# Attribute groups loaded further ahead, and edge rows added by VectorE: a graph pipeline on one core

## The reference

```
edge_in = concat(h[row], h[col], edge_attr)            # 256 + 256 + 64
msg     = relu(edge_in @ W1.T + b1) @ W2.T + b2
agg     = segment_sum(msg, row)
h'      = GRU(agg, h)                                  # W_ih, W_hh, b_ih, b_hh
x       = x + h'
```

## Time and profile before

| | us |
|---|---|
| median of 3 runs | 9225.33 (9208.56 to 9230.66) |
| the profiled execution, its own time | 9230.41 |
| its span in the trace | 9228.7 |
| TensorE busy | 5520.2 (60% of the span) |
| VectorE busy | 4108.1 (45%) |
| GpSimd busy | 4089.5 (44%) |
| ScalarE busy | 1858.0 (20%) |
| mean granted TensorE clock | 0.774 of full |

### The profile page before, as it was taken

How to read it: one execution, slowest core, us unless ns; L and a number is a source line. 1 busy time by engine, 2 the same in 40 slices (tenths; PEclk the granted TensorE clock), 3 DMA queues, 4 the chain that set the end, 5 groups by cost and what they waited for, 6 DMA issues and landing times. The chain is left out here.

```text
span 9228.7 us, 92213 instructions
## 1 busy us (share of the span) xinstructions
PE 5520.2 (60%) x22602; PEld 3755.3 (41%) x22603; DVE 4108.1 (45%) x11767; ACT 1858.0 (20%) x3938; POOL 4089.5 (44%) x3696
## 2 busy tenths in 40 slices
PE   2666477666557656658894665429964554553562
PEld 1344355455434434445552444325642232232551
DVE  9000577655631244444455777871133343343003
ACT  1222000011111122222112444312321221120120
POOL 5763466577646648870002444200016636642331
PEclk9999788777668877779796777658986676675785
DMA  2443111233325467760001222100013323320552
GB/s 52 86 87 87 37 22 20 48 97 98 79 86 153 132 102 138 138 126 1 8 10 49 62 60 62 31 1 14 14 35 89 90 51 92 89 62 15 169 170 91
DMA packets 495939, 657.70 MB, mean 71 GB/s; under 512 B 177294, under 2 KB 378098, under 8 KB 495669
## 3 DMA queue, kind: packets, MB, share of 16 engines
q0 software_dynamic: 229440, 352.40, 18.0%
q1 hardware_dynamic: 266228, 302.44, 11.0%
HBM read 512.00 MB, written 141.59 MB: 71 GB/s over the span
## 5 line engine op out<-in xcount | busy, mean ns | idle before, releaser
L739 POOL DMA_INDIRECT conv_rows<-rows_b,end_dst x832 | 837.2, 1006 | 1517.4 <-SPq L2406 1147.3
L771 DVE TENSOR_TENSOR acc<-acc,ps 125x256 f32 (+2 forms) x2080 | 881.3, 424 | 1199.7 <-issue 370.6
L739 POOL DMA_INDIRECT gat_rows<-rows,end_dst x832 | 869.1, 1045 | 627.3 <-issue 233.0
L2452 PE MATMUL ps<-conv_rows,conv_weight_of 128*125 128x256 f32 x1664 | 629.6, 512 | 674.9 <-issue 310.0
L739 POOL DMA_INDIRECT hyp_rows<-rows,end_dst x416 | 415.1, 998 | 993.7 <-SPq L1967 492.5
L1581 POOL DMA_INDIRECT mpnn_rows<-rows_b,end_src x416 | 657.4, 1580 | 261.7 <-DMA mpnn_rows<-records_src 139.5
L2452 PEld LDWEIGHTS ps<-conv_rows,conv_weight_of 128*125 128x125 f32 x1664 | 346.1, 239 | 958.4 <-issue 519.8
L1298 PE MATMUL ps<-xT,experts_w 128*128 128x500 f32 (+1 forms) x1344 | 560.7, 555 | 186.2 <-DMA experts_w<-in_L_ffn_w 162.2
L309 POOL DMA_INDIRECT records_src<-by_src_edge_stage,by_src_edge_slot x400 | 521.3, 1303 | 336.6 <-DMA by_src_edge_stage<-edge_rows 224.1
L474 POOL DMA_INDIRECT records_dst<-front_back,front_dst_addr x400 | 494.9, 1237 | 269.4 <-issue 269.4
L878 DVE TENSOR_REDUCE gat_red<-ps 125x8 f32<-125x1024 f32 x416 | 503.9, 1217 | 197.0 <-remote 127.8
(11 more groups left out here) (559 smaller groups left out, 9886.9 us busy)
## 6 DMA issues: line engine op xcount, KB each, us to landing
mlp_w<-in_L_ffn_w SPq DMA_DIRECT2D x136, 512.0 KB
mpnn_rows<-records_src SPq DMA_DIRECT2D x52, 1024.0 KB
edge_rows<-front_edge_ring SPq DMA_DIRECT2D x100, 503.9 KB
by_src_edge_stage<-edge_rows SPq DMA_DIRECT2D x100, 503.9 KB
gat_rows<-rows,end_dst POOLq DMA_INDIRECT x832
conv_rows<-rows_b,end_dst POOLq DMA_INDIRECT x832
front_attr<-in_edge_attr SPq DMA_DIRECT2D x100, 125.0 KB
rows_b<-acc SPq DMA_DIRECT2D x3, 3125.0 KB
```

Of the source, the lines that this page charges most:

```text
L739: pool.indirect_dma_start(out=rows[:, n % U, t, :], out_offset=None, in_=table, in_offset=bass.IndirectOffsetOnAxis(ap=ends[:, n * G + t:n ...
L771: dve.tensor_tensor(here, here, S.ps[0:P, t % banks, 0:width], ALU.add).then_inc(added, 1)
L2452: pe.matmul(S.ps[0:P, t, 0:D], weight_of[:, q.slot, t, :], rows[:, q.slot, t, :], start=True, stop=True).then_inc(summed, 1)
```

## The change

In the front part the attribute buffers go from 3 to AR = 6 and the ring from 2 to ER = 3. SyncE loads group g + 6 ahead of the store of group g, not group g + 3 behind it.

In the message loop the edge rows have a buffer of their own, `mpnn_edge`, of two halves of four tiles (512 KB each in a transfer); there are two loads a group, each waiting for `joined` of the same half of the group before. GpSimd uses `gather_groups` and adds nothing; it no longer waits for edge rows. VectorE's message t adds the product to the edge buffer. Behind each four messages a new stage, `join`, adds the edge half to the gathered rows (128 x 4 x 256), and ScalarE's relu waits for the join. SyncE no longer waits for the memsets (`ready`) before its first load.

```diff
--- before.py
+++ after.py
@@ -153,6 +153,8 @@
 SC = EC + PADC
 SG = 4
 AG = 4
+AR = 6
+ER = 3
 
 
 def turning(nc, S, A, sb, names):
@@ -378,10 +380,10 @@
             sem(x) for x in ("keys_ready", "staged", "scattered", "back_in", "taken"))
 
 
-        attr, attr_t = sb("attr", [P, 3, AG, ED]), sb("attr_t", [ED, 2, AG, P])
-        ring = sb("edge_ring", [P, 2, AG, EW])
-        attr_in = [sem(f"attr_in{r}") for r in range(3)]
-        rows_stored = [sem(f"edge_rows_stored{r}") for r in range(2)]
+        attr, attr_t = sb("attr", [P, AR, AG, ED]), sb("attr_t", [ED, 2, AG, P])
+        ring = sb("edge_ring", [P, ER, AG, EW])
+        attr_in = [sem(f"attr_in{r}") for r in range(AR)]
+        rows_stored = [sem(f"edge_rows_stored{r}") for r in range(ER)]
         attr_turned, attr_out, edge_product, edge_out = (
             sem(x) for x in ("attr_turned", "attr_out", "edge_product", "edge_out"))
         w1c = turned["L1_gnn_W1"][0:ED, 4, :]
@@ -406,7 +408,7 @@
                 for dst_, src_ in loads[:len(TURNED)]:
                     sp.dma_start(dst_, src_).then_inc(loaded, 16)
                 attributes = A["edge_attr_64"].rearrange("(p t) c -> p t c", p=P)
-                for g in range(3):
+                for g in range(AR):
                     sp.dma_start(attr[:, g], attributes[:, g * AG:(g + 1) * AG, :]).then_inc(attr_in[g], 16)
                 sp.dma_start(S.x[:, :, :], A["x"].rearrange("(t p) d -> p t d", p=P)).then_inc(x_in, 16)
                 sp.dma_start(w[:], A["L0_gnn_W"].rearrange("(k p) f -> p k f", p=128)).then_inc(gat_in, 16)
@@ -420,12 +422,12 @@
 
                 out = S.edge_rows.rearrange("(p t) w -> p t w", p=P)
                 for g in range(AGROUPS):
+                    if g + AR < AGROUPS:
+                        sp.wait_ge(attr_turned, g + 1)
+                        sp.dma_start(attr[:, g % AR], attributes[:, (g + AR) * AG:(g + AR + 1) * AG, :])\
+                            .then_inc(attr_in[g % AR], 16)
                     sp.wait_ge(edge_out, 3 * (g + 1))
-                    sp.dma_start(out[:, g * AG:(g + 1) * AG, :], ring[:, g % 2]).then_inc(rows_stored[g % 2], 16)
-                    if g + 3 < AGROUPS:
-                        sp.wait_ge(attr_turned, g + 1)
-                        sp.dma_start(attr[:, g % 3], attributes[:, (g + 3) * AG:(g + 4) * AG, :])\
-                            .then_inc(attr_in[g % 3], 16)
+                    sp.dma_start(out[:, g * AG:(g + 1) * AG, :], ring[:, g % ER]).then_inc(rows_stored[g % ER], 16)
                 sp.wait_ge(blocks_copied, len(jobs))
                 for to, from_ in stores:
                     sp.dma_start(to, from_).then_inc(stored, 16)
@@ -438,8 +440,8 @@
                 sp.wait_ge(back_in, 16)
                 sp.wait_ge(nodes_stored, 32)
                 sp.wait_ge(stored, 16 * len(stores))
-                for r in range(2):
-                    sp.wait_ge(rows_stored[r], 16 * AGROUPS // 2)
+                for r in range(ER):
+                    sp.wait_ge(rows_stored[r], 16 * len(range(r, AGROUPS, ER)))
 
             @block.gpsimd
             def _(pool):
@@ -491,11 +493,11 @@
 
                 for g in range(AGROUPS + 1):
                     if g < AGROUPS:
-                        pe.wait_ge(attr_in[g % 3], 16 * (g // 3 + 1))
+                        pe.wait_ge(attr_in[g % AR], 16 * (g // AR + 1))
                         if g >= 2:
                             pe.wait_ge(attr_out, g - 1)
                         for t in range(AG):
-                            ins = pe.transpose(S.ps[0:ED, g % 2, t * P:(t + 1) * P], attr[:, g % 3, t, :],
+                            ins = pe.transpose(S.ps[0:ED, g % 2, t * P:(t + 1) * P], attr[:, g % AR, t, :],
                                                S.ident[0:P, 0:P])
                         ins.then_inc(attr_turned, 1)
                     if g >= 1:
@@ -549,13 +551,13 @@
                            .then_inc(attr_out, 1)
                     if g >= 1:
                         h = g - 1
-                        if h >= 2:
-                            act.wait_ge(rows_stored[h % 2], 16 * (h // 2))
+                        if h >= ER:
+                            act.wait_ge(rows_stored[h % ER], 16 * (h // ER))
                         at = slice(h * AG, (h + 1) * AG)
-                        act.copy(ring[:, h % 2, :, 0:2], stage[:, at, 0:2]).then_inc(edge_out, 1)
+                        act.copy(ring[:, h % ER, :, 0:2], stage[:, at, 0:2]).then_inc(edge_out, 1)
                         for t in range(0, AG, 2):
                             act.wait_ge(edge_product, 2 * h + t // 2 + 1)
-                            act.copy(ring[:, h % 2, t:t + 2, 2:EW],
+                            act.copy(ring[:, h % ER, t:t + 2, 2:EW],
                                      S.ps[0:P, 2 + 2 * (h % 2) + t // 2, :].rearrange("p (t d) -> p t d", d=D))\
                                .then_inc(edge_out, 1)
 
@@ -1547,10 +1549,10 @@
                 dve.wait_ge(taken, 2)
 
         gathered = [sem(f"gathered{u}") for u in range(U)]
-        edges_in = [sem(f"edges_in{u}") for u in range(U)]
-        (go, selected, turned, turned_out, widened, products, messages, rectified, summed, added, ready) = (
-            sem(x) for x in ("go", "selected", "turned", "turned_out", "widened", "products", "messages", "rectified",
-                             "summed", "added", "ready"))
+        edges_in = [sem(f"edges_in{u}") for u in range(2)]
+        (go, selected, turned, turned_out, widened, products, messages, joined, rectified, summed, added, ready) = (
+            sem(x) for x in ("go", "selected", "turned", "turned_out", "widened", "products", "messages", "joined",
+                             "rectified", "summed", "added", "ready"))
         with nc.Block() as block, ExitStack() as ctx:
             def mb(what, shape, dt=F32):
                 return ctx.enter_context(nc.sbuf_tensor(f"mpnn_{what}", shape, dt))
@@ -1558,30 +1560,24 @@
             rows = mb("rows", [128, U, G, D + 1])
             onehot_b, onehot = mb("onehot_b", [128, 2, G, P], BF16), mb("onehot", [128, 2, G, P])
             onehot_t = mb("onehot_t", [P, 2, G, 128], BF16)
+            edge = mb("edge", [128, 2, G // 2, D])
             view = S.records["src"].rearrange("(p t) w -> p t w", p=128)
 
             PB = 4
 
             @block.sync
             def _(sp):
-                sp.wait_ge(ready, 2)
-
                 def load(q):
-                    if q.since(U):
-                        sp.wait_ge(summed, (q.n - U + 1) * G)
-                    sp.dma_start(rows[:, q.slot, :, 0:D], view[:, q.tiles(), 2:EW]).then_inc(edges_in[q.slot], 16)
+                    for half in range(2):
+                        if q.since(1):
+                            sp.wait_ge(joined, 2 * q.n - 1 + half)
+                        tiles = bass.ds(q.n * G + half * (G // 2), G // 2)
+                        sp.dma_start(edge[:, half], view[:, tiles, 2:EW]).then_inc(edges_in[half], 16)
                 pipeline(sp, (0, load))
 
             @block.gpsimd
             def _(pool):
-                for n in range(GROUPS):
-                    pool.wait_ge(edges_in[n % U], 16 * (n // U + 1))
-                    pool.sem_inc(go, 1)
-                    for t in range(G):
-                        pool.indirect_dma_start(
-                            out=rows[:, n % U, t, 0:D], out_offset=None, in_=S.rows_b,
-                            in_offset=bass.IndirectOffsetOnAxis(ap=ends[:, n * G + t:n * G + t + 1], axis=0),
-                            compute_op=ALU.add).then_inc(gathered[n % U], 16)
+                gather_groups(pool, ends, S.rows_b, rows[:, :, :, 0:D], summed, gathered, go)
 
             @block.vector
             def _(dve):
@@ -1597,17 +1593,30 @@
 
                 def message(t):
                     def stage(q):
-                        if t == 0:
-                            dve.wait_ge(gathered[q.slot], rows_in(q))
+                        half, m = t // (G // 2), t % (G // 2)
+                        if m == 0:
+                            dve.wait_ge(edges_in[half], 16 * (q.n + 1))
                         dve.wait_ge(products, q.n * G + t + 1)
-                        v = rows[:, q.slot, t, 0:D]
+                        v = edge[:, half, m, :]
                         dve.tensor_tensor(v, v, S.ps[:, 2 + t % PB, 0:D], ALU.add).then_inc(messages, 1)
                     return stage
 
+                def join(half):
+                    def stage(q):
+                        if half == 0:
+                            dve.wait_ge(gathered[q.slot], rows_in(q))
+                        at = slice(half * (G // 2), (half + 1) * (G // 2))
+                        dve.wait_ge(messages, q.n * G + at.stop)
+                        v = rows[:, q.slot, at, 0:D]
+                        dve.tensor_tensor(v, v, edge[:, half], ALU.add).then_inc(joined, 1)
+                    return stage
+
```

(10 more changed lines are left out.)

## The result

| | before | after | after / before |
|---|---|---|---|
| first chip, median of 4 runs each, us | 9220.2 (9208.6 to 9230.7) | 8962.7 (8932.4 to 8980.2) | 0.9718 (0.9687 to 0.9748) |
| span of the profiled execution, us | 9228.7 | 8978.5 | |

The change takes 257 us off by the medians, 250 by the two traces, where 169 were forecast (9056 us; 8975 was the range's lower end). By the traces, 179 us are gained by the time the first graph layer starts (65 were forecast), 35 of them are gone again at that layer's end, the message loop gains 96 (104 were forecast), and what follows gains some 10.

The account below looks back on a forecast made before the run. The prediction took five nearly full DMA engines to bound the front loop and GpSimd's adding gathers the message loop. From 9230.4 us, -65 (front) and -104 (message loop) gave 9061, or 9056 against the median; range 8975 to 9165.

Parts of the forecast that it names:

- Work on the queue is unchanged: Front loop: five full DMA engines still need 665 us, or 686 at 97% busy, where the loop took 740.
- The term: Front loop: loading ahead of the store makes it 65 us shorter, taken from a range of 54 to 75.
- Rival 3: Front loop: load latency, not the queue, bounds it; scatters' end then binds; at most 164 us less, about 8957; chance 0.08.
- five engines 97% busy: Front loop: the five DMA engines used by 125-partition transfers are 90% busy on average, 97% at the best.
- T: Message loop: length of one step after the change, taken as 13.5 us, between 12.4 and 15.3.
- a pair: Message loop: one message and accumulate on VectorE, 0.76 us at the full TensorE clock, 1.38 at half.
- A fall of the clock: Message loop: TensorE's granted clock falling in a step costs about 2.9 us; expected in some of the steps.
- rival 2: Message loop: the clock falls each step, T = 15.3; with the front's 65 us less, about 9148; chance 0.13.
- the 11.5 to 12.5: Message loop: us of GpSimd gathers a group, 10.0 for plain gathers plus blocking by the joins.
- The edge loads: Message loop: a half's load takes 4.5 to 5 us, hidden by 7.6 us of VectorE work.
- Rival 4: Message loop: plain gathers put VectorE in a slow pace, T = 18.4, about 9306 us against the median; chance 0.07.

Follow-up runs that it names:

- front_only: The change's front part with the message loop of before: 8672.2 us beside 8846.5 for the kernel before, ratio 0.9812.
- changed_again: The changed kernel, unaltered, run once more on a faster chip: 8483.1 us beside 8835.2 for the kernel before, ratio 0.9602.

## Why the prediction was wrong

- *Which side, and which engine.* Faster was right. The message loop was bound by GpSimd, as said. In the front loop TensorE waited for the load, as said, but that wait was laid to a nearly full queue, and that was wrong.
- *The step that failed*: "Work on the queue is unchanged: 0.281 x 16 x 740 us / 5 = 665 us of five full engines." I took the time that packets took for work that has to be done. It holds waiting inside of packets too. The 63 MB take 44.6 us of engine time a megabyte in the changed kernel, where transfers are always queued, and that makes 5.6 us a group and not 6.65 to 6.9. The term was -65. It measured -168 at the load behind the scatters, -179 when the first graph layer starts, and -174 as a part of its own (front_only). It is the whole of the miss: with it, 9225 - 168 - 96 = 8961 against the median, and 8963 was measured.
- *Rival 3* had the size right (8957) with half of the mechanism. It called the load's latency the limit, which the circle bears out, and let TensorE bind next, at 4.81 us; the queue bound next, at 5.6. The part that decided its sum held: the load of what the scatters wrote is tied to their end, 807.2 us in the rival and 803 measured. I gave it 0.08, against the evidence of "five engines 97% busy", which is the same misreading. The trace of before had the argument against a full queue, the circle of 8.3 and 5.4 us, which gives the pace without any full queue; I looked at shares only.
- *The message loop*: -104 forecast, -96 measured on the first chip, T = 13.5 forecast, 13.1 on average between all selects. That this came so near is luck in part: single terms were off and made up for each other. At the full clock a pair takes 0.66 us, not 0.76, probably because TensorE's products run ahead during the joins, and the step is 11.1, not 12.4 (changed_again). A fall of the clock costs 12.7 - 11.1 = 1.6 us, not 2.9. On the first chip the clock fell in each of the 42 steps, which was the condition of rival 2 and not a fall in some steps, and the step was 13.3 and not its 15.3. What 12.7 leaves to 13.3 goes with the pauses of that kind of chip. On a chip without them T is 11.8 and the gain 179.
- *GpSimd*: 1.172 us and 0.30 a gather make 11.8 us a group, within the 11.5 to 12.5, but by another sum: it is blocked by the select as well as by the joins.
- *The edge loads* are hidden, as said: one wait of 4.5 us in the loop.
- *Rival 4*'s row was real, but plain gathers are not its cause, since the faster chips have the same gathers without it; it did not come with this change. The range (8975 at the low end) missed the 8963 by 12 us.

## What to carry to other kernels

The busy share of a DMA queue isn't the work that it has to do: before calling it full, look at megabytes in a unit of time and for a circle of waits, issue to landing to the next issue, that gives the same pace. Where transfers of different length go through one queue, the short one that an engine waits for belongs ahead of the long one; that order alone gave what three more buffers gave. When an addition moves from a DMA to VectorE, count its blocking of GpSimd with the selects that already do the same, and look at which wait ends last once GpSimd is faster: here it was ScalarE's order, and moving one line of it was worth 68 us on one kind of chip and nothing on the other.
